# Perceiver block on one core: the context's columns kept on chip, its chunks run one iteration ahead, four state sums made by TensorE and not by GpSimd

## What is computed

```python
# 1: latent attention; each query looks at a window of 9 keys around its segment
kv_c = kv @ W_kvc;  q_c = q @ W_dq                       # kv: the context
good = (k_ids <= qs) & (k_ids >= qs - LOOKBACK)
attn = softmax(where(good, scores, NEG));  out = attn @ v  # no good key: the mean over all keys
# 2: state-space layer, 512 channels x 16 states
h = dA_t * h + dBx_t                                     # scan over 128 positions, per state s
y = einsum('bles,bls->ble', hs, Cm) + xc * Dp
# 4: cross attention over the whole context, keys and values rounded to integers
kv = (cond @ Wkv + bkv);  s = max(|k|, per head) / 127;  k = round(k / s)
attn = softmax(q @ k.T);  attn = round(attn * 255 / max);  out = attn @ v
```

## Time and profile before

| | |
|---|---|
| median of 3 runs | 495.3 us (493.67 to 495.8) |
| profiled execution, time of its own | 492.2 us |
| profiled execution, span of the core | 490.4 us |
| TensorE clock granted, mean of the span | 0.962 of full |
| busy, of the span | PE 85%, DVE 76%, ACT 64%, POOL 28% |
| windows and mean, first sublayer | 0 to 88.7 us |
| weights and setup of the state layer | 88.7 to 120.3 us |
| loop of eight iterations | 120.3 to 214.0 us |
| the rest, cross attention most of it | 214.0 to 490.4 us |

### The profile page before, as it was taken

How to read it: one execution, slowest core, us unless ns; L and a number is a source line. 1 busy time by engine, 2 the same in 40 slices (tenths; PEclk the granted TensorE clock), 3 DMA queues, 4 the chain that set the end, 5 groups by cost and what they waited for, 6 DMA issues and landing times.

```text
span 490.4 us, 9583 instructions
## 1 busy us (share of the span) xinstructions
PE 418.6 (85%) x3919; PEld 318.3 (65%) x3959; DVE 370.8 (76%) x577; ACT 311.8 (64%) x397; POOL 135.4 (28%) x182
## 2 busy tenths in 40 slices
PE   8889629895999899889966998899899989878897
PEld 4778528672665555446643777777777777765586
DVE  5437720485899999976787999999999999823443
ACT  2343413248777777624567999999999999951120
POOL 4145500206466666600002333332111111100000
PEclk9999868998899999999995999999999999989999
DMA  8866850502122221027197444445554444000000
GB/s 301 328 274 197 104 215 1 215 1 88 64 66 64 64 67 64 1 86 318 46 393 303 173 175 172 173 194 216 217 235 178 173 173 174 1 3 0 1 0 22
DMA packets 14966, 67.94 MB, mean 139 GB/s; under 512 B 6170, under 2 KB 9034, under 8 KB 11850
## 3 DMA queue, kind: packets, MB, share of 16 engines
q1 hardware_dynamic: 14346, 63.79, 35.4%
q0 software_dynamic: 576, 3.54, 1.9%
HBM read 66.16 MB, written 1.15 MB: 137 GB/s over the span
## 4 chain that ended last, share of the span: by engine, by line
DVE 34%; PE 29%; issue 15%; DMA 10%; ACT 6%; POOL 5%; POOLq 0%; SPq 0%; DVEq 0%; ACTq 0%
DVE arena L1301 15%; DVE w L1301 7%; DMA arena<-in_context 4%; DVE arena L1311 4%; PE ps L1619 4%; PE ps L1910 3%; POOL vrow L620 3%; DVE arena L1192 2%; PE ps L1626 2%; DMA arena<-arena 2%; DMA arena<-ks_scr 2%; DMA arena<-in_rope,arena 2%; PE ps L1536 2%; PE ps L1730 1%; PE ps L1602 1%
## 5 line engine op out<-in xcount | busy, mean ns | idle before, releaser
L1301 DVE CUSTOM_DVE_ANT_0 arena<-ps,arena 128x1024 f32<-128x1024 f32 x88 | 108.3, 1280 | 0.7 <-PE ps L1790 0.6
L1790 PE MATMUL ps<-arena 128*128 128x512 bf16 x216 | 69.3, 387 | 22.4 <-DVE arena L1301 18.8
L1818 PEld LDWEIGHTS ps<-cst,arena 128*128 128x128 f32 x512 | 64.7, 143 | 27.4 <-ACT arena L967 2.3
L1818 PE MATMUL ps<-cst,arena 128*128 128x128 f32 x512 | 79.6, 280 | 3.1 <-ACT arena L976 3.1
L962 ACT ACTIVATE arena<-arena 128x4096 uint8<-128x4096 f32 x21 | 78.0, 3713 | 5.4 <-POOL arena L703 5.2
L1831 PE MATMUL ps<-vrow,arena 128*128 128x16 f16 x1024 | 60.5, 169 | 0.0
L1831 PEld LDWEIGHTS ps<-vrow,arena 128*128 128x128 f16 x1024 | 54.1, 97 | 1.6
L976 ACT ACTIVATE arena<-ps 128x512 f32<-128x512 f32 x95 | 49.6, 586 | 6.4 <-PE ps L1831 3.4
L1301 DVE CUSTOM_DVE_ANT_0 w<-ps,arena 128x1024 f32<-128x1024 f32 x40 | 49.6, 1279 | 3.1 <-DMA arena<-ks_scr 3.1
L699 POOL TENSOR_SCALAR arena<-arena 128x1 f32<-128x1 f32 x32 | 11.8, 368 | 138.2 <-DVE arena L1301 138.2
L1830 PE MATMUL ps<-vrow,arena 128*128 128x16 f16 x760 | 49.8, 170 | 0.0
(11 more groups left out here) (271 smaller groups left out, 754.8 us busy)
## 6 DMA issues: line engine op xcount, KB each, us to landing
arena<-ks_scr SPq DMA_DIRECT2D x16, 2048.0 KB, 8.1
arena<-in_context SPq DMA_DIRECT2D x16, 512.0 KB, 3.4
arena<-in_w SPq DMA_DIRECT2D x1, 4488.0 KB, 13.7
w<-in_w SPq DMA_DIRECT2D x1, 2927.0 KB, 13.9
arena<-in_w0b SPq DMA_DIRECT2D x1, 2560.0 KB, 10.9
arena<-in_w SPq DMA_DIRECT2D x1, 2048.0 KB, 8.3
arena<-bc_scr SPq DMA_DIRECT2D x16, 128.0 KB, 3.5
arena<-in_fill SPq DMA_DIRECT2D x1, 2048.0 KB, 7.4
```

Of the source, the lines that this page charges most:

```text
L1301: dve.tensor_tensor_reduce(s_sb[slot][:, keys], ps[:, 2 * (c % 2):2 * (c % 2) + 2, :].rearrange("p a n -> p (a n)"), ksb[h % 2][:, keys], ...
L1790: mm = pe.matmul(bank(2 * (c % 2) + m, 0, 512), qz[h // 8][:, h % 8, b * L:(b + 1) * L], kT[:, h // 8, k:k + 512], start=True, stop=True)
L1818: mm = pe.transpose(bank(4 + n % 3, k * P, P), words[:, w:w + P], ident)
```

## The change

The context comes a second time as an argument, laid out with its columns on partitions (`in_columns`), and is loaded once, in four transfers, into the place of `vT` (later the values overwrite it chunk by chunk). `turned`, `context_columns`, the chunk loads and GpSimd's adding up are gone; the mean comes from four ScalarE copies with an accumulated sum (`mean`, 128x2048 each). The mean's latent is written by ScalarE into row 0 of `kvg`, so its transfer is gone. `w1` is now issued ahead of the nine transfers of `kvg`. Chunk 0 is made inside the first sublayer, chunk 1 ahead of the loop, and iteration `i` makes chunk `i+2`. In iterations 1, 3, 5 and 6 TensorE makes both sums. The first weights come in two halves, and layer norm's columns go first.

```diff
@@ constants
+SUMS_PE = (1, 3, 5, 6)
@@ SyncE
-            sp.wait_ge(pe_step, WABS)
             sp.wait_ge(got_rope[1], 16)
-            chunk(0)
-            chunk(1)
+            for b in range(B):
+                for c in range(CH):
+                    sp.dma_start(vT[:, c, b * NKEY:(b + 1) * NKEY], columns_d[:, c, b * NKEY:(b + 1) * NKEY]).then_inc(ld_cT, 16)
             sp.dma_start(w0b[:, :], w0b_d).then_inc(ld_w0b, 16)
-            for c in range(2, 6):
-                chunk(c)
             key_rows(0)
-            chunk(6)
-            chunk(7)
             key_rows(1)
+            sp.dma_start(w1[:, :], w1_d).then_inc(ld_w1, 16)
             sp.wait_ge(st_kv, 32)
             for j in range(WIN):
-                sp.dma_start(kvg[j * GQ:(j + 1) * GQ, :, :], ...
+                sp.dma_start(kvg[1 + j * GQ:1 + (j + 1) * GQ, :, :], ...
-            sp.dma_start(w1[:, :], w1_d).then_inc(ld_w1, 16)
-            sp.wait_ge(kvm_ready, 2)
-            sp.dma_start(kvg[GK:GK1, :, :], kvm[:, :, :]).then_inc(ld_kvg, 16)
@@ GpSimd
-            for c in range(NC): ... pool.tensor_tensor(csums[:, b], ..., cs[:, c % 2], ALU.add) ...
             for i in range(NC - 1):
                 input_of(i + 1, 0)
-                scales_of(i + 1)
+                if i + 2 < NC:
+                    scales_of(i + 2)
                 input_of(i + 1, 1)
-                sum_of(i)
+                if i not in SUMS_PE:
+                    sum_of(i)
@@ ScalarE
+            def mean(b, c):
+                act.wait_ge(ld_cT, 16 * B * CH)
+                keys = vT[:, c, b * NKEY:(b + 1) * NKEY]
+                act.activation(keys, keys, ACT.Copy, accum_out=mT[:, CH * b + c:CH * b + c + 1]).then_inc(means, 1)
+            def values_of(i, m):
+                act.wait_ge(v_ps, 2 * i + 2)
...
+            integers(0)
+            for m in range(CH):
+                values_of(0, m)
             columns(1)
...
             for i in range(NC - 1):
-                context_columns(i + 1)
                 decay(i + 1, 0)
-                key_columns(i)
+                key_columns(i + 1)
                 decay(i + 1, 1)
-                for m in range(CH):
-                    values_of(i + 1, m)
-                integers(i + 1)
+                if i + 2 < NC:
+                    for m in range(CH):
+                        values_of(i + 2, m)
+                    integers(i + 2)
@@ VectorE
             for i in range(NC):
                 scan(i, 0)
                 scan(i, 1)
                 read_out(i, 0)
+                if i + 2 < NC:
+                    key_maxima(i + 2)
+                read_out(i, 1)
+                if i + 2 < NC:
+                    scaled_keys(i + 2)
                 if i + 1 < NC:
-                    key_maxima(i + 1)
-                read_out(i, 1)
-                if i + 1 < NC:
-                    scaled_keys(i + 1)
-                largest(i)
+                    largest(i + 1)
@@ TensorE, first sublayer
             weighted_latents(0)
             weighted_latents(1)
-            prob_columns(4)
-            prob_columns(5)
             attended(0)
-            prob_columns(6)
-            prob_columns(7)
+            keys(0)
+            for n in range(4, 8):
+                prob_columns(n)
             weighted_latents(2)
             weighted_latents(3)
             attended(1)
+            values_of(0, 0)
+            values_of(0, 1)
@@ TensorE, loop
             for i in range(NC - 1):
-                turned(i + 1)
-                key_columns(i)
-                keys(i + 1)
-                values_of(i + 1, 0)
-                values_of(i + 1, 1)
+                key_columns(i + 1)
+                if i + 2 < NC:
+                    keys(i + 2)
+                    values_of(i + 2, 0)
+                    values_of(i + 2, 1)
                 first_sum(i)
+                if i in SUMS_PE:
+                    sum_of(i, 1, hc[:, 1].rearrange("p t n -> p (t n)")).then_inc(hc_used[1], 1)
                 read_rows(i + 1)
```

More of the change, by code:

```diff
@@ L64 @@
 KT_AT = 25880
+VT_AT = KT_AT + KEYS
+HALF_A = H // 2 * (QC + KVC)
 UNITS = B * H
 LAST = UNITS - 1
-def adds(c):
-    per = NC // B
-    return c // per * (per + 1) + max(c % per, 1)
+SUMS_PE = (1, 3, 5, 6)
 class Chain:
@@ L152, in perceiver_kernel @@
         phase()
-        w_uqT = take([H, QC])
-        w_ukT = take([H, KVC])
+        w_abs = [(take([H // 2, QC]), take([H // 2, KVC])) for _ in range(2)]
         w_kvcT = take([D])
@@ L196, in perceiver_kernel @@
         phase()
-        cs = take([2, CT, D])
-        phase()
-        kvm = take([NG, KVC], rows=1)
+        krow = take([B, WIN, 2 * KVC])
+        assert at[0] <= W0A
+        phase(qall_at)
+        w_vo = take([PAIRS, D])
         taken = [0]
@@ L549, in _ @@
             sp.wait_ge(st_bc, 16)
-            for n in range(4):
+            for n in range(DS):
                 inputs(n)
-            context(1)
-            for i in range(1, NC):
-                if i + 1 < NC:
-                    context(i + 1)
-                if 2 * i + 3 < DS:
-                    inputs(2 * i + 2)
-                    inputs(2 * i + 3)
             sp.wait_ge(th_done, 2)
@@ L1429, in _ @@
                 mm = pe.matmul(bank(7, 0, T, 0, QC), w_dq[:, c, :], xnT[:, c, :], start=(c == 0), stop=(c == CH - 1))
+            mm.then_inc(pe_step, 1)
+            absorbed(1)
+            for c in range(CH):
+                mm = pe.matmul(bank(6, c * R, R), w_kvcT[0:KVC, c * P:(c + 1) * P], w_kr[0:KVC, :], start=True, stop=True)
             mm.then_inc(pe_step, 1)
@@ L1502, in weights_vo @@
                 mm.then_inc(wvo, 1)
-            def mean_column(b):
-                pe.wait_ge(csum, (b + 1) * (NC // B + 1))
-                for c in range(CH):
-                    mm = pe.matmul(bank(7, 8 + CH * b + c, 1), csums[:, b, 0, c * P:(c + 1) * P], ones[:, 0:1], start=True, stop=True)
-                return mm
             def prob_columns(n):
@@ L2012 @@
         "context": a["ctx_2048"].reshape(KEYS, D),
+        "columns": rows(a["ctx_2048"].reshape(KEYS, D).T),
         "rope": rope, "cst": cst, "w0a": w0a, "w0q": w0q, "w0b": w0b, "w1": w1, "w2": w2, "w3": w3,
```

340 lines of the change are left out of this document (157 added, 183 removed).

## The result

| | before | after |
|---|---|---|
| median, same chip | 494.5 us (4 runs) | 481.35 us (479.4 to 482.35, 4 runs) |
| ratio | | 0.9735, 95% interval 0.968 to 0.979 |
| profiled execution, its span | 492.2, 490.4 us | 480.45, 478.4 us |
| busy, of the span | PE 85%, DVE 76%, ACT 64%, POOL 28% | PE 87%, DVE 76%, ACT 65%, POOL 22% |

The change makes the kernel 13 us faster in the medians and 12.0 us in the profiled spans.

A forecast was written before the change was run, and what follows sets the result against it. It took one transfer queue to bound the first sublayer and VectorE the loop, TensorE close behind. 7.4 us at the first scan plus 3.7 in the loop made 11.1, so 484.2 us in the median, range 479 to 490.

The forecast's parts named there:

- Part 1, 12.1 us earlier, 59.0: First sublayer: weighted latents start at 59.0 us instead of 71.1, when the nine `kvg` transfers have landed.
- `kvg` is quicker: Rival, first sublayer: nine transfers queued behind `w1` take 6.6 us, not 9.4; iteration 0 may stay warm; 479.7 us, chance 0.18.
- putting `w1` ahead of `kvg` costs its 7.1 us here: First sublayer's queue: `w1` delays the latents by its 7.1 us, but pays by making chunk 0 possible.
- Part 2, 7.4 us at the first scan: Latents to state layer: the loop's first scan comes at 112.9 us instead of 120.3.
- The 17.1 in the 21.2: Latents to last projection's end: 17.1 us as before plus 4.1 for `keys(0)`, so it ends at 80.2.
- Part 3, the loop, 3.7 us: Loop: iteration 0 loses 1.1 us, iterations 1 to 5 save 1.0, iterations 6 and 7 save 3.8.
- the ring over ScalarE: Loop: keys, values, evictions, integers, transposes make 11.5 us, so iterations 2 and 4 save 0.5 each, not 1.3.
- The end won 3.98 (3.8): Loop iterations 6 and 7: no chunk made in 6, scans without the sum; 3.8 us saved.
- The rest, 276.4 within 1: From last read-out to the end: 276.4 us as before, within 1; the prediction is wrong if this stretch changes.
- Loads of 360 or 303 GB/s: Rival, first sublayer: long loads are slower; at 360 the time is 488 us, chance 0.12; at 303, 493, chance 0.06.
- TensorE as the loop's bound: Rival, loop: waits between engines add 0.5 us to six iterations, iteration 6 gains half; 4.5 us lost, 488.5, chance 0.08.
- No cold clock came in the loop: Rival, loop: TensorE's clock falls; with a third of its work cold the time is 511 us, chance 0.04.

The follow-up runs named there:

- w1_behind: Changed kernel with the load of `w1` issued behind the nine `kvg` transfers, as in the kernel before: 477.8 us, ratio 0.964 to the kernel before.
- awake_latents2: Changed kernel with 18 matmuls without use in TensorE's wait for the nine `kvg` transfers: 478.3 us, ratio 0.963 to the kernel before.
- awake_gap: Changed kernel with 34 matmuls without use in TensorE's idle time before iteration 0: 476.5 us, ratio 0.961 to the kernel before.
- before_sums: Kernel before the change, with only odd sums 1, 3, 5 and 6 moved to TensorE: 496.0 us, ratio 1.003.
- sums_gpsimd: Changed kernel with all seven odd sums on GpSimd, chunks still running ahead: 488.8 us, ratio 0.987 to the kernel before.
- combined2: Changed kernel with `w1` behind the nine transfers, `keys(0)` behind the second pair of latents, 34 useless matmuls before iteration 0: 474.6 us, ratio 0.958.
- combined_full2: combined2 plus integers ahead of the values' evictions and all seven odd sums on TensorE: 476.0 us, ratio 0.962 to the kernel before.

## Why the prediction was right, step by step

**Part 1, 12.1 us earlier, 59.0.** Measured 57.4, so 13.7. The bound was named rightly: the latents wait for the nine transfers, and ScalarE's mean is done at 54.4 (timeline below), hidden by 3 us rather than 5.

```profile
52.53 1.90 ACT L779 ACTIVATE arena<-ps 1x1024 f32<-1x1024 f32 x2
```

Two terms were off, in opposite directions. The long loads moved 409 GB/s and not 420, and 37 to 42 us, with the two stores, only 219, so `w1` had landed at 51.4 (GpSimd's first cast of it) and not at 49.6. But the nine took some 7 us behind it, 50 to 57, and not 9.4, by luck as short as in the rival "`kvg` is quicker", whose full engines did not come: the share stayed at 0.71. They were issued from 42.7 on, under `w1`, and were alone only from 50. Alone, as in w1_behind, 9.4 is about right (64 GB/s). And "putting `w1` ahead of `kvg` costs its 7.1 us here" was wrong: it costs 3.3 (w1_behind), since the sum gave the nine the same 9.4 us in either place. Wrong too was that it "pays": w1_behind makes chunk 0 in the same place of TensorE's order and has its first scan 1.9 us earlier, with 477.8 us in the median. `w1` did not fill the wait for the stores either: some 2.7 of its 3.0 MB moved after 42 us (an estimate from the 347 GB/s of 42 to 50). On the page weighed there, the Trainium skill's "DMA: Bandwidth & Descriptors", Specifications, with 358 GB/s for a core: the trace does not agree, with 409 over 16 us.

**Part 2, 7.4 us at the first scan.** Measured 8.9; the 1.5 us more are part 1's. From the latents to the end of `attended(1)` it took 22.0 and not 21.2 us; the way from there to the input projection 5.4 and not 5.7, so the values and their evictions cost 0.9 us, not 1.3; the setup 26.7 and not 27.0. The 17.1 in the 21.2 had been taken over from a stretch that was itself cold in part, without saying so: warm it is 2.9 us less (awake_latents2). The text named the low clock in its first paragraph and then priced it only in iteration 0.

**Part 3, the loop, 3.7 us.** Measured 4.24 (93.64 to 89.40). Iteration 0 loses 1.18 (1.1 predicted), by a cold clock, as awake_gap shows. The pitches won 1.44 (1.0 predicted): 0.56 in iterations 2 and 4, bound by the ring over ScalarE and TensorE's list as said, and 0.15 in iterations 3 and 5, where the first scan of a pair takes 3.40 and not 3.55. The end won 3.98 (3.8). The waits of 0.63 us in iterations 2 and 4 were predicted as at most 0.8. What the prediction did not see is how the parts lean on each other: it priced a sum at 1.3 us of VectorE's time, one by one. before_sums shows the sums alone to lengthen the loop; the chunks alone lengthen it too (sums_gpsimd), but by the cold iteration 0 and one dip of the clock.

**The rest, 276.4 within 1.** Measured 277.5, so just outside, and by its own last sign the prediction fails in this one point. The kernel loses an estimated 1.7 us in the window from 446.4 (10 us at 0.83); the same matmuls before, some 13 us later, stood in a window with 1.00. Nothing of the change lies there, and the kernels of the table have 275.6 to 279.1 for this stretch. That scatter, like the two clocks of combined2 and combined_full2, is not explained.

**The sum.** In the spans 12.0 us were won and not 11.1: 8.9 and 4.2, less 1.1 behind the loop. The median is 2.9 us under the forecast; 0.9 of it is this. The rest is that the median stood 3.1 us above the profiled execution before and 0.9 after, where the prediction took 3.1 for both; no run explains it.

**The rivals.** Loads of 360 or 303 GB/s did not come. TensorE as the loop's bound did not cost 4.5 us, though at 11.5 us it is what keeps more from being won. No cold clock came in the loop after iteration 0; it did come once in sums_gpsimd, behind an idle time of 2.0 us, for 0.85.

## What to carry to other kernels

Price a stretch together with the clock it ran at: durations taken from a cold stretch carry the cold with them, and the cheapest gains here (2.1 and some 2 us) were matmuls without use in two waits of 4 and 8 us. When work moves from an engine that blocks another to the engine that is nearly full, look for what stands behind it there: four sums on TensorE are worth 5.8 us (0.85 of it one dip of the clock) in a loop whose other work had been taken off TensorE, and cost 2.0 in one where it had not. And before a transfer is said to delay those behind it by its length, look when these could have been issued, how they move alone (`w1`, 7.1 us long, cost 3.3), and what stands right behind them, here the mean.

## What the runs showed of the hardware

- VectorE's scan and GpSimd's addition, both on 128x1024 in SBUF, do not run side by side: they took turns, 7.95 us for two scans of 2.2 and 4.33 for a sum of 2.36 (sums_gpsimd).
- After an idle wait of 4.0 us (changed kernel) TensorE ran at a granted clock of 0.51 (58 to 62 us) and 0.82 (62 to 70); after 7.8 us at 0.75 over 13 us. With matmuls in the wait it was 1.00 (awake_latents2, awake_gap). But it was also 0.57 to 0.59 in 58 to 62 us of w1_behind and combined_full2 with no idle time over 1 us just before, and 1.00 in combined2 with the same order. What decides there stays open.
- Nine transfers of 64 KB in small pieces left the engines at a share of 0.70 to 0.73 while they were alone: 64 GB/s before (52 to 58 us) and in w1_behind (44 to 46), 70 in the changed kernel (50 to 54).
